# A hybrid block of two attentions and two feed-forwards: the seam between the first feed-forward and the second attention reordered

## The reference

```python
x = x + _L0_attn_a_ref(_layernorm(x), ...)     # 2 heads of 64, rotary, bias
x = x + _L0_ffn_ref(_layernorm(x), ...)        # 128 -> 512 -> 512 -> 512 -> 128
x = x + _L0_attn_b_ref(_layernorm(x), ...)     # 16 heads of 8, masked
x = x + _L0_ffn_ref(_layernorm(x), ...)        # the same weights again

# feed-forward
h = silu(tlin(x, w1)) * tlin(x, w2)
h = gelu(tlin(h, h1)); h = gelu(tlin(h, h2)); return tlin(h, w3)     # tlin: product, then a scale per output

# second attention
qkv = encodings @ attn_w.T + attn_b
scores = einsum('bhki,bhqi->bhkq', k, q) / sqrt(8)
probs = softmax(where(k_index <= q_index, scores, -10000), axis=k)
out = einsum('bhkq,bhkl->bhql', probs, v);  return out @ out_w.T + out_b
```

## Time and profile before

| | us |
|---|---|
| median of three runs | 689.67 (687.04 to 690.79) |
| the profiled execution | 687.75 |
| its span, first to last instruction | 685.9 |
| PE busy in the span | 644.3 (94%) |
| DVE / ACT / POOL busy | 482.2 / 440.5 / 419.3 |
| PE busy from 304 to 306, 310 to 312, 313 to 314 | 1.41 of 2, 0.66 of 2, 0.00 of 1 |

### The profile page before, as it was taken

The page is one execution under the profiler, slowest core; times in us unless marked ns, Lnnn a source line. Parts: engine busy times, 40 slices in busy tenths (PEclk is TensorE's granted clock), DMA queues, the critical chain, the costliest instruction groups (busy, mean ns, idle before and its releaser), DMA issues.

```text
span 685.9 us, 14286 instructions
## 1 busy us (share of the span) xinstructions
PE 644.3 (94%) x4816; PEld 460.7 (67%) x4816; DVE 482.2 (70%) x948; ACT 440.5 (64%) x776; POOL 419.3 (61%) x452
## 2 busy tenths in 40 slices
PE   6899998989999999998999999988988999999997
PEld 4566665768787776674565665655556877787785
DVE  5677787845676587467899899987677855577411
ACT  4588867556656665555767767766854666656664
POOL 2564536677878776443464565555648786777773
PEclk8999999999999999999999999999999999999999
DMA  7333334000000002631666675662320000000001
GB/s 215 89 73 83 74 72 46 1 2 0 1 0 0 0 1 92 215 125 54 227 195 213 225 242 194 239 226 73 97 79 19 0 16 15 15 15 1 16 16 32
DMA packets 35589, 56.61 MB, mean 83 GB/s; under 512 B 5072, under 2 KB 10192, under 8 KB 35536
## 3 DMA queue, kind: packets, MB, share of 16 engines
q1 hardware_dynamic: 35264, 55.53, 26.6%
q10 hardware_dynamic: 272, 0.39, 0.2%
HBM read 27.08 MB, written 24.38 MB: 75 GB/s over the span
## 4 chain that ended last, share of the span: by engine, by line
PE 68%; DVE 10%; ACT 9%; issue 6%; DMA 3%; POOL 3%; ACTq 0%; SPq 0%; DVEq 0%; POOLq 0%
PE banks L232 64%; ACT b_prob L1618 4%; DVE xn L185 3%; PE banks L224 2%; ACT a_prob L625 1%; ACT xn L208 1%; DVE f_gate L1156 1%; PE banks L1041 1%; DVE f_hidden L1163 1%; ACT f_g_hi L1112 1%; DVE f_h_hi L1160 1%; DVE b_segment_max L1730 1%; PE banks L493 1%; DMA b_o_dram<-b_o 1%; POOL rstd L219 1%
## 5 line engine op out<-in xcount | busy, mean ns | idle before, releaser
L1227 POOL TENSOR_TENSOR f_g_lo<-f_gelu,f_g_hi 128x512 fp32r<-128x512 f32 x127 | 162.9, 1292 | 54.9 <-ACT f_g_hi L1112 54.4
L1111 ACT ACTIVATE f_gelu<-banks,cols 128x512 f32<-128x512 f32 x128 | 88.3, 690 | 128.9 <-PE banks L232 106.0
L1851 POOL TENSOR_SCALAR_AFFINE_SELECT b_prob<-b_prob 128x512 f32<-128x512 f32 x128 | 81.7, 640 | 86.5 <-ACT b_prob L1618 85.8
L1730 DVE TENSOR_REDUCE b_segment_max<-banks 128x6 f32<-128x768 f32 x128 | 118.8, 948 | 20.2 <-PE banks L232 19.6
L232 PE MATMUL banks<-f_g_hi,whi 128*128 128x512 f32 x320 | 130.2, 407 | 1.9 <-POOL f_g_lo L1227 1.4
L1618 ACT ACTIVATE b_prob<-banks 128x768 f32<-128x768 f32 x128 | 102.5, 808 | 42.4 <-PE banks L232 42.0
L232 PE MATMUL banks<-f_g_lo,whi 128*128 128x512 f32 x320 | 126.7, 396 | 0.0
L1220 POOL TENSOR_TENSOR f_h_lo<-f_hidden,f_h_hi 128x512 fp32r<-128x512 f32 x60 | 77.6, 1294 | 58.3 <-DVE f_hidden L1163 50.2
L232 PE MATMUL banks<-f_h_hi,whi 128*128 128x512 f32 x256 | 104.8, 409 | 3.9 <-ACT f_g_hi L1112 3.2
L232 PE MATMUL banks<-f_h_lo,whi 128*128 128x512 f32 x256 | 102.4, 400 | 0.0
L1112 ACT ACTIVATE f_g_hi<-banks,cols 128x512 fp32r<-128x512 f32 x128 | 87.4, 683 | 0.0
(11 more groups left out here) (142 smaller groups left out, 1070.1 us busy)
## 6 DMA issues: line engine op xcount, KB each, us to landing
f_h_hi<-b_q_dram SPq DMA_DIRECT2D x16, 512.0 KB, 4.1
f_h_lo<-b_k_dram SPq DMA_DIRECT2D x16, 512.0 KB, 5.2
b_o_dram<-b_o SPq DMA_DIRECT2D x8, 1024.0 KB, 4.3
b_q_dram<-b_q_hi SPq DMA_DIRECT2D x16, 256.0 KB, 3.3
b_k_dram<-b_k_hi SPq DMA_DIRECT2D x16, 256.0 KB, 2.9
w_stage<-in_wF SPq DMA_DIRECT2D x8, 352.0 KB, 3.5
b_q_dram<-b_q_lo SPq DMA_DIRECT2D x8, 256.0 KB, 3.6
b_k_dram<-b_k_lo SPq DMA_DIRECT2D x8, 256.0 KB, 3.2
```

The costliest lines, as they stand in the source:

```text
L1111: nc.scalar.activation(gf[c % 2][:, :], z_bank[c % 2], ACT.Gelu, scale=scale).then_inc(s_gf, 1)
L1227: nc.gpsimd.tensor_tensor(lo[:, c, :], gf[c % 2][:, :], hi[:, c, :].bitcast(F32), ALU.subtract).then_inc(s_glo[c % 2], 1)
L1730: nc.vector.reduce_max(seg[:, g, s, 2 * p:2 * p + 2, :], first_pass[:, 2 * p:2 * p + 2, 0:3 * P].rearrange("p b (c k) -> p b c k", c=3), A ...
L1851: nc.gpsimd.affine_select(out=pr, in_=pr, compare_op=ALU.is_ge, fill=0.0, base=0, pattern=[[0, 4], [1, P]], channel_multiplier=-1).then_in ...
```

## The change

Four things are moved; nothing is computed otherwise.

1. TensorE's value projection of block 0 goes from chunk 0 to chunk 1 of "second" in the feed-forward's block 6.
2. ScalarE's negation and store of block 0's first maxima go from chunk 2 to chunk 1 of "second" in block 7.
3. ScalarE's scaling of the last down product goes from the end of step 0 of the attention's block 0 to directly behind that step's first exponential, ahead of the second half's negative maxima, of the second exponential and of the maxima's DMA.
4. The norm of block 2 leaves step 0 of the attention. VectorE's statistics stand behind the second reduction pair of block 7 (chunk 1 of "first"), GpSimd's two operations behind its chunk 2, and VectorE's norm is spread, one tile behind each of the four reduction pairs of "second".

```diff
-            def dve_apply(self, dve, b, first):
+            def dve_apply(self, dve, b, first, tiles=range(TILES)):
...
-                for s in range(TILES):
+                for s in tiles:
@@ pe_front, block LAST - 1
-                    if at == "second" and c == 0:
+                    if at == "second" and c == 1:
                         pe.wait_ge(s_lo, 2)
                         pe_v(pe, FIRST_BLOCK)
@@ act_body of the second attention
                     act_exp(act, b, n, 0)
+                    if is_block(b, 0) and n == 0:
+                        prev["act_tail"](act)
                     if not one and n == MAX1_AT + 1:
                         act_max_rows(act, b, 1)
...
-                    if is_block(b, 0) and n == 0:
-                        prev["act_tail"](act)
@@ act_front
-                if is_block(b, LAST) and (at, c) == ("second", 2):
+                if is_block(b, LAST) and (at, c) == ("second", 1):
                     act_max(act, FIRST_BLOCK, 0)
                     act_max_rows(act, FIRST_BLOCK, 0)
@@ dve_body of the second attention
-                    if is_block(b, 0) and n == 0:
-                        norm.dve_stats(dve, n2)
-                    elif two and n == 0:
+                    if two and n == 0 and not is_block(b, 0):
                         norm.dve_apply(dve, n2, False)
...
-                    if is_block(b, 0) and n == 0:
-                        norm.dve_apply(dve, n2, False)
@@ dve_front, block LAST
                     dve_first(dve, FIRST_BLOCK, c, (1, 0))
+                    if c == 1:
+                        norm.dve_stats(dve, FIRST_BLOCK.after(2))
...
                     for n in range(HALF, STEPS):
                         dve_first(dve, FIRST_BLOCK, n, (1, 0))
+                        norm.dve_apply(dve, FIRST_BLOCK.after(2), False, (n - HALF,))
@@ pool_body of the second attention
-                    if is_block(b, 0) and n == 0:
-                        norm.pool(pool, b.after(2))
@@ pool_front
+                if is_block(b, LAST) and (at, c) == ("first", 2):
+                    norm.pool(pool, FIRST_BLOCK.after(2))
```

## The result

| | before | after |
|---|---|---|
| median (range), four executions each | 688.94 us (687.04 to 690.79) | 680.55 us (680.21 to 680.87) |
| ratio, 95% interval | | 0.9877 (0.9849 to 0.9905) |
| profiled execution / its span | 687.75 / 685.9 | 680.26 / 678.5 |
| mean granted clock in the profiled execution | 0.989 | 0.998 |
| changed kernel once more, eight executions | 688.15 (686.05 to 691.01) | 683.4 (680.92 to 686.0), ratio 0.9925 (0.9898 to 0.9951) |

The changed kernel is faster. Eight more executions of the same file gave 4.8. All twelve together have a mean of 682.4, and 80 executions of before have a mean of 688.4, so about 6.0 is what the change is worth.

A forecast was written before the change was run, and what follows sets the result against it. TensorE, busy 94% of the span, was taken as the bound. 1.44 - 0.26 + 0.19 + 2.6 + 1.3 = 5.3, less 0.1, gave 5.2 us off the median 689.67: 684.5, range 681.5 to 689.

The forecast's parts named there:

- value projection: Block 6: moving it a chunk later removes TensorE's wait for `b_k_lo`; gain 1.44 us, bounds 0.8 and 1.44.
- statistics of block 2: Last feed-forward block: they start VectorE's third reduction 0.29 us late; cost to TensorE 0.26, bounds 0 and 0.5.
- first maxima: Last feed-forward block: issuing their DMA a chunk sooner starts the last Gelu earlier; gain 0.19 us, bounds 0 and 0.2.
- waits for `f_yT` and `xn`, with what is next: Second attention's start: gaps 1.34 and 1.53 us vanish, 0.25 new wait; gain 2.6, less 0.1 for the held second exponential.
- clock: Slow stretch behind 315 us, blamed on TensorE's poor filling from 310 to 315, goes; gain 1.3 us, bounds 0 and 1.3.
- Norm a tile at a time: Last feed-forward block: a tile behind each second-half reduction costs nothing, hidden in VectorE's idle time or under `pe_down`.
- Scaling: Attention's step 0: run behind the first exponential, it removes TensorE's 1.34 us gap; step 1 then waits some 0.25.
- The second rival: Behind the attention's first steps the slow clock stretch comes all the same: gain 3.9 us, 685.8; chance 0.17.
- Front gain eaten: Rival: rows land late or VectorE's reduction loop costs over 0.26 us; gain 3.6 to 4, 685.9; chance 0.12.
- New wait: Rival: exponentials and maxima behind the scaling on ScalarE's queue hold TensorE's step 1; gain 2.4 us, 687.3; chance 0.11.
- Slower through the maxima's transfer: Rival: steady blocks wait longer for the maxima's DMA as loads meet in another order; 3.3 us slower, 693; chance 0.06.
- The level: Whole kernel: forecast set against the median 689.67 us, 1.9 above the profiled execution, giving 684.5 instead of 682.6.

The follow-up runs named there:

- edit 2 alone: Kernel before with only ScalarE's negation and DMA of the first maxima a chunk sooner: 686.24 us, a single execution.
- filled: Kernel before with 5 and 6 useless matmuls in TensorE's gaps before the transpositions of `f_yT` and `xn`, waits kept: 687.27 us, ratio 0.9976.
- edit 1 alone: Kernel before with only the value projection moved by a chunk: 687.3 us, ratio 0.9982.
- edit 4 alone: Kernel before with only block 2's norm moved into the last block of the feed-forward: 685.88 us, ratio 0.9963.
- edit 3 alone: Kernel before with only the scaling moved behind the first exponential: 685.81 us, ratio 0.9974.

## Why the prediction was right or wrong

| term of the sum | forecast | measured | where |
|---|---|---|---|
| value projection | 1.44 | 1.70 | A |
| statistics of block 2 | -0.26 | -0.16 | B |
| first maxima | 0.19 | 0.00 | C, edit 2 alone |
| waits for `f_yT` and `xn`, with what is next | 2.6 - 0.1 | 2.80 | rest of D's gain |
| clock | 1.3 | 1.34 | behind the transposition of `xn`, before less filled |
| sum | 5.2 | 5.67 | |

**Bound and places.** Right. TensorE's own sequence set the time, and the edits paid where it stood.

**Value projection.** Right in mechanism, and too small by 0.26. I took the idle time of the row, 1.44, which counts from a modelled matmul end. The starts tell more: from the transposition at 268.40 to the projection it was 2.04, and in the changed kernel it is 0.36 from that transposition to the matmul that now follows it. That is 1.68 of the 1.70. The same is behind the 2.80 against 2.5 in D: start to start the two gaps gave back 1.50 and 1.71 instead of 1.34 and 1.53, while the steps behind them, which now wait for exponentials, took 0.36 and 0.18 more. The doubt about the rows' landing was the right one to have (0.62 us late in the trace of edit 1 alone), and so was the cover.

**Statistics.** The third reduction came 0.21 later (forecast 0.29), and that cost TensorE 0.16 instead of 0.26. The bounds held it.

**Norm a tile at a time.** Cost nothing, as forecast: C is the same with and without it. A tile took 0.34, where I had expected 0.46 beside GpSimd. Three of the four tiles ran while GpSimd wrote `f_g_lo`, as this one of VectorE and GpSimd's operation around it:

```profile
297.55 0.34 DVE L185 TENSOR_SCALAR xn<-X,mv,rstd 128x128 f32<-128x128 f32 x1
```

```profile
296.51 1.30 POOL L1227 TENSOR_TENSOR f_g_lo<-f_gelu,f_g_hi 128x512 fp32r<-128x512 f32 x1 [1.92 <-ACT f_g_hi L1112]
```

So the 0.1 us a tile that I had put down to GpSimd, and had said the trace bears out, isn't borne out by these. In the kernel with edit 4 alone one tile of the four took 0.50.

**First maxima.** Here a step failed. ScalarE did come to its last Gelu at once, and TensorE's wait fell by 0.18. But I wrote that all that waits for the Gelu gains it, and didn't ask what TensorE's next wait was. It was VectorE's last reduction, in the same place to 0.01 us before and after.

**Scaling.** Right. `f_yT` starts at 305.63 with the negative maxima behind it, its transposition has no wait, and the step after it waits 0.35 for the second exponential (0.25 forecast).

**Clock.** Right in this case and priced right against the one trace. Three more traces with both gaps had the fall too, at up to 0.91 more, so my upper bound of 1.3 was too low. In the seven traces with neither gap there is none. The second rival, that it falls all the same, didn't come.

**The rivals.** Front gain eaten: no, A and B give 1.54 where 1.18 was forecast. New wait: only the 0.35. Slower through the maxima's transfer: behind D the profiled pair differs by 0.01 us. Between two executions of one file the part behind D differs by 1.7 us (before) and 1.8 us (changed), so a small effect there could hide.

**The level.** This is the step that failed and put the result outside the range: not a term of the gain, but the level it was set against, and with it the lower bound. The sum was made against the profiled execution and gave 682.6, and the mean of twelve executions of the changed kernel is 682.4. Then I added the 1.9 between that execution and the median of three, and reached down to 681.5 only. Both treat the spread of before, 687.04 to 690.79, as if the changed kernel could only be shifted with it. It is chance of two kinds: where the clock falls, and how long the part behind D takes (365.9 to 368.4 us in thirteen traces), for which the transfers are the likely but unproven reason. I had read the clock at 316 and not at 8 and at 142, where before was slow in code that no edit touches. Had I done so, I would have seen that 1.83 us of the profiled execution could be absent in the next one. 687.75 less 5.2, less these 1.83, is 680.7, so the range had to reach to 680, which takes in all four executions of after. That the first four came so near to each other and so low is chance as far as the runs show: eight more of the same file spread over 5.1 us.

**What stays open.** How the spread divides exactly. In the traces, the five with the fall near 141 come 2.4 us later to block 6 in the mean than the seven others, a fall in D costs up to 2.3 us, and the part behind D varies by 2.5 us without the clock: the longest, 368.4 (edit 3 alone), has a mean granted clock of 1.00 there. What sets that last part isn't shown. Open is also whether the changed kernel's gain is nearer 5 or nearer 8, which the intervals of its two measurements (6.5 to 10.4, and 3.4 to 7.0) hardly settle. The sum of the parts, 5.67, and the pooled 6.0 lie between.

## What to carry to other kernels

Read a gap from start to start of the matmuls around it, and when a wait is shortened, look up what the very next instruction waits for before you count the gain: here 0.18 us of a visible wait was worth 0.00. Lay two traces out over stretches between instructions that both have, the part ahead of the first edit included; what differs there is chance, and belongs in the range on both sides. And where TensorE stands idle between dense stretches, price the clock behind the gap beside the gap itself: filling two gaps with matmuls that compute nothing brought 1.43 us in the trace here, 1.34 of it from the clock.

## What the runs showed of the hardware that was not expected

- A gap of 1.93 us ahead of dense matmuls, in identical code, was followed by half clock in five traces and by full clock in seven. One gap of 1.34 us (edit 4 alone) sufficed for it in one trace.
- A fall of the clock in D made it 1.4 us longer than with the gaps filled in two traces and 2.2 to 2.3 us in two others (D less 9.76).
- A norm tile (128x128, f32) on VectorE took 0.34 us between reductions, beside a busy GpSimd and beside an idle one, while four in a row at 270.30 took 0.46 each.
- The first DMA that ScalarE issues for the maxima took 1.11 us of its queue, also when moved a chunk ahead; the second took 0.55:

```profile
297.08 1.11 ACTq L1637 DMA_DIRECT2D f_h_hi<-b_negative_max  x1
...
306.82 0.55 ACTq L1637 DMA_DIRECT2D f_h_hi<-b_negative_max  x1
```
